# Two small bias arrays in front of x in place of in front of the slope: 64 bytes of shift for x, both weight halves, the stage and the identity

## What is computed

```python
Wc = conv_w[:, :, 0, 4]
def step(prev, x_i):
    y = jnp.einsum('oc,nch->noh', Wc, prev) + conv_b[None, :, None]
    y = jnp.where(y >= 0, y, prelu_a * y)
    cur = y + x_i
    return (cur, cur)
x = jnp.moveaxis(feature, 3, 0)
_, fwd_rest = jax.lax.scan(step, x[0], x[1:])
fl = jnp.concatenate([x[0:1], fwd_rest], axis=0)
_, bwd_rest = jax.lax.scan(step, fl[-1], fl[:-1], reverse=True)
```

## The kernel before

| tensor | remainder by 128 | remainder by 512 |
|---|---|---|
| `x_sb`, `w_hi` (and `pairs` in its place), `w_lo` (and `w_raw`), `stage`, `ident` | 0 | 128 |
| `a_scale`, `a_shift`, `g_scale`, `g_shift` | 0 | 128, 256, 384, 0 |
| `s_hi`, `s_lo`, `act_buf` | 64 | 320, 320, 320 |
| `unit`, `cent`, `gated_mean` (statistics) | 0 | 0, 256, 128 |
| `group_ones`, `ones_bf` | 96 | 96 |

## Time and profile before

### The profile page before, as it was taken

How to read it: one execution, slowest core, us unless ns; L and a number is a source line. 1 busy time by engine, 2 the same in 40 slices (tenths; PEclk the granted TensorE clock), 3 DMA queues, 4 the chain that set the end, 5 groups by cost and what they waited for, 6 DMA issues and landing times.

```text
span 852.3 us, 13842 instructions
## 1 busy us (share of the span) xinstructions
PE 828.0 (97%) x4060; PEld 661.3 (78%) x4060; DVE 660.5 (77%) x1461; ACT 421.1 (49%) x1401; POOL 66.7 (8%) x106
## 2 busy tenths in 40 slices
PE   7788899999999999999999999999999999999998
PEld 6743478888888888888888888888888888888887
DVE  6978877777767676676766788888888888888887
ACT  6874455444454445444454444544445444554445
POOL 8963300000000000000000000000000000000000
PEclk9999999999999999999999999999999999999999
DMA  9940200000000000000000023332333223332233
GB/s 381 417 193 0 100 26 0 1 0 0 0 0 0 0 0 0 0 0 0 0 0 0 15 84 98 98 91 62 94 98 98 82 65 98 98 98 73 75 98 99
DMA packets 70654, 56.34 MB, mean 66 GB/s; under 512 B 1904, under 2 KB 66416, under 8 KB 68720
## 3 DMA queue, kind: packets, MB, share of 16 engines
q1 hardware_dynamic: 70640, 56.17, 19.8%
HBM read 39.39 MB, written 16.78 MB: 66 GB/s over the span
## 4 chain that ended last, share of the span: by engine, by line
PE 87%; DVE 4%; DMA 3%; ACT 3%; SPq 1%; issue 1%; DVEq 0%; ACTq 0%
PE ps_prods L706 27%; PE ps_prods L700 26%; PE ps_prods L703 26%; PE ps_turns L722 6%; DMA x_sb<-x_cols 3%; SPq L306 1%; DVE below_flags L1061 1%; ACT stage L541 1%; ACT stage L517 1%; ACT ps_turns L481 1%; DVE cells L1078 0%; ACT w_hi L512 0%; PE ps_values L652 0%; ACT ps_prods L481 0%; PE ps_group L663 0%
## 5 line engine op out<-in xcount | busy, mean ns | idle before, releaser
L700 PE MATMUL ps_prods<-w_hi,s_hi 128*128 128x512 f32 x990 | 397.1, 401 | 0.0
L703 PE MATMUL ps_prods<-w_lo,s_hi 128*128 128x512 f32 x990 | 394.7, 399 | 0.0
L706 PE MATMUL ps_prods<-w_hi,s_lo 128*128 128x512 f32 x990 | 387.6, 392 | 0.0
L551 ACT ACTIVATE act_buf<-ps_prods 128x256 f32<-128x256 f32 x247 | 81.8, 383 | 338.1 <-PE ps_prods L706 333.0
L1167 DVE SCALAR_TENSOR_TENSOR x_sb<-act_buf,x_sb 128x256 f32 (+1 forms) x247 | 105.1, 426 | 143.7 <-ACT act_buf L558 133.7
L706 PEld LDWEIGHTS ps_prods<-w_hi,s_lo 128*128 128x128 f32 x990 | 186.4, 188 | 35.6
L700 PEld LDWEIGHTS ps_prods<-w_hi,s_hi 128*128 128x128 f32 x990 | 186.1, 188 | 33.5
L703 PEld LDWEIGHTS ps_prods<-w_lo,s_hi 128*128 128x128 f32 x990 | 186.5, 188 | 31.1
L558 ACT ACTIVATE act_buf<-ps_turns,bias 128x128 f32<-128x128 f32 x494 | 156.7, 376 | 49.5 <-PE ps_turns L722 49.5
L564 ACT ACTIVATE ps_below<-ps_turns,neg_bias 128x128 f32<-128x128 f32 x494 | 152.1, 361 | 0.0
L1174 DVE SCALAR_TENSOR_TENSOR x_sb<-ps_below,neg_slope,x_sb 128x256 f32 (+1 forms) x247 | 118.8, 481 | 5.4
(11 more groups left out here) (208 smaller groups left out, 369.2 us busy)
## 6 DMA issues: line engine op xcount, KB each, us to landing
stage<-x_cols SPq DMA_DIRECT2D x31, 512.0 KB, 3.9
out_cols<-x_sb SPq DMA_DIRECT2D x31, 512.0 KB, 4.6
x_sb<-x_cols SPq DMA_DIRECT2D x15, 1024.0 KB, 18.5
w_raw<-w_t SPq DMA_DIRECT2D x8, 512.0 KB, 19.1
x_sb<-x_cols SPq DMA_DIRECT2D x1, 2048.0 KB, 8.0
x_sb<-x_cols SPq DMA_DIRECT2D x2, 512.0 KB, 27.3
out_cols<-x_sb SPq DMA_DIRECT2D x4, 128.0 KB, 2.1
params<-gates SPq DMA_DIRECT2D x1, 60.0 KB, 14.2
```

The source lines that it names most:

```text
L551: act.activation(act_buf[:, half], ps_prod[c if bank is None else bank][:, half], ACT.Copy) .then_inc(raw_copied, 1)
L700: pe.matmul(out, s_hi[:, k, :], w_hi[:, k, w_cols], start=(k == 0), stop=False)
L703: pe.matmul(out, s_hi[:, k, :], w_lo[:, k, w_cols], start=False, stop=False)
L706: return pe.matmul(out, s_lo[:, k, :], w_hi[:, k, w_cols], start=False, stop=(k == CT - 1))
```

## The change

Two lines move: `bias` and `neg_bias`, 32 bytes per partition each, are allocated ahead of `x_sb` and no longer behind `g_shift`. Everything that lay between the two places starts 64 bytes higher: `x_sb`, `pairs`, `w_hi`, `w_raw`, `w_lo`, `stage`, `ident` and the four scale and shift arrays. What comes behind `neg_bias` (the slopes, all `tmp` tiles, `s_hi`, `s_lo`, `act_buf`) keeps its address. No instruction, wait, loop or transfer is added, removed or put elsewhere in its queue.

```diff
@@ -71,6 +71,8 @@
             return ctx.enter_context(nc.semaphore(name))
 
 
+        bias = sb("bias", [P, CT])
+        neg_bias = sb("neg_bias", [P, CT])
         x_sb = sb("x_sb", [P, CT, COLS, NH])
         pairing = ExitStack()
         pairs = pairing.enter_context(nc.sbuf_tensor("pairs", [P, 4 * C + P], fp32))
@@ -87,8 +89,6 @@
         a_shift = sb("a_shift", [P, N, CT])
         g_scale = sb("g_scale", [P, N, CT])
         g_shift = sb("g_shift", [P, N, CT])
-        bias = sb("bias", [P, CT])
-        neg_bias = sb("neg_bias", [P, CT])
         slope = sb("slope", [P, 1])
         neg_slope = sb("neg_slope", [P, 1])
         rest_slope = sb("rest_slope", [P, 1])
```

## The result

| | before | changed |
|---|---|---|
| median | 854.12 us (4 runs) | 863.46 us (862.14 to 863.55, 4 runs) |
| profiled execution | 854.0 us | 862.14 us |
| span | 852.3 us | 860.4 us |
| TensorE busy | 828.0 us | 835.8 us |

The change makes the kernel slower by 1.05% (ratio 1.0105, 95% interval 1.0092 to 1.0118). The forecast was 854.1, range 853.3 to 855.4. The profiled execution of the changed kernel is the shortest of its four: it is 8.1 us longer than the one before, where the medians are 9.3 apart. What follows accounts for the 8.1; the other 1.2 us no trace shows.

A forecast was written before the change was run, and what follows sets the result against it. The prediction took TensorE's count of scan matmuls by their distance as the bound. All four terms were zero (DMA -0.31 to +0.35, moving side -1.24 to +1.24), so it forecast the median, 854.1 us, range 853.3 to 855.4.

The forecast's parts named there:

- What bounds the kernel: In the 62 scan steps, some 738 us, time is the count of matmuls by their distance, 229 ns each.
- TensorE, stationary side: Weight loads and warm-up matmuls: remainders and a different distance between the operands cost zero; loads take 188 ns at each remainder.
- TensorE, moving side: Scan matmuls reading weights now at remainder 64: zero, bounded by a 0.42 ns clock pulse each, 1.24 us either way.
- The bf16 row: Nearest trace row: ones_bf at remainder 96, 216 ns between matmuls, so an off-line moving start costs at most 2 to 3 ns.
- the unexplained 13 ns: In each scan matmul, 229 ns is 13 ns more than bf16's 216; the trace doesn't say of what, taken as zero.
- Rival A: Slower: each of 2970 scan matmuls pays for a split line of the moving read; 856.6 from two pulses; chance 0.07.
- Rival C: Faster: the 192 over 512 start suits the scan's moving read better, 851.6 or less from two pulses; chance 0.07.
- Rival B: Slower: load pieces of x cut finer, deciding from 1.7 us or 19 ns a piece; 856 to 857; chance 0.04.
- VectorE, GpSimd, ScalarE: Their accesses to x, stage, state and w_lo cost zero at any remainder; L1142 stays at 426 ns.
- DMA: Load of x: zero, with -0.31 to +0.31 us for 64 bytes (2.4 ns) a piece; last store 0.04 us.
- The rule weighed in the prediction: Load of x: transactions start on multiples of 256 bytes, so the shift wastes two more beats, 0.31 us, giving 854.4.
- The cover of 0.34 us a step: In the scan, the path through ScalarE and VectorE may grow 0.34 us a step before TensorE waits.

The follow-up runs named there:

- e2_x_not_w: Kernel before with bias and neg_bias ahead of x_sb, slopes ahead of w_hi: x at remainder 64, weights at 0 by 128; 866.24 us, ratio 1.0139.
- e4_state_too: Changed kernel with a 64-byte gap ahead of s_hi, so weights and state keep the distance of the kernel before; 854.37 us, ratio 1.0.
- first probe: Kernel before plus 48 groups of 40 float32 matmuls of 512 columns behind the warm-ups, operand starts varied; 226.7 to 234.1 ns a matmul.
- second probe: Kernel before plus 25 groups of 40 matmuls with varied operand offsets, types and columns; bf16 216 ns, plain float32 112 ns a matmul.

## Why the prediction was wrong, point by point

*What bounds the kernel.* Right. The time is the number of matmuls by the time between their starts: 12.033 less 11.907 us a step explains 7.8 of the 8.1 us of the profiled executions.

*TensorE, stationary side.* Here is the step that failed: "The price of a different distance between the operands is zero by these rows." I named the very quantity and dismissed it by 188 against 188 ns and 394 against 395. Those are durations, and durations did not move in the slow kernel either. The fault is one that the front of this text warns of: the rate is in the starts. Nor was "the scan's stationary operand does not move anyway" a reason: its distance to the moving one did. Nor could the eight warm-ups have told. They lie at distance 0, the best one, but behind the first their starts are 225 to 236 ns apart, 231.5 in the mean, more than the scan's 229 at distance 64; a stream may need its first six matmuls to settle.

*TensorE, moving side.* This is the term of the sum that was mis-sized: I took zero with bounds of one clock pulse, 1.24 us, and it was 7.8 us. The 3.4 ns between 228.9 and 232.3, eight pulses, act on the 40 of a step's 48 matmuls that stand apart from the transposes: 0.136 us, against the 0.126 by which the step grew, so the rest of the step, around the transposes, gives a little back. The bf16 row was no neighbour: bf16 is indifferent to what costs float32 up to 7.4 ns. And the unexplained 13 ns over the bf16 distance were the hint: two of them go away at distance 0 in the probe.

*Rival A* had the place (each matmul of the scan), the sign of the result and its mark in the profile (steps of 11.92 us or more, all else in place), at a chance of 0.07. Its cause, a split line of the moving operand, is refuted by e2_x_not_w and e4_state_too. *Rival C* was right that the present layout is not the best, by 0.5%, but the moving operand's own start is not what counts, and the place that C named, 192 over 512 with the state where it is, is the slower one. *Rival B* has a slip in its price: the load is 128 pieces in a row, so 1.7 us would be 13 ns a piece and not 19.

*VectorE, GpSimd, ScalarE.* Right where seen: L1142 stays at 426 ns, and L439's median goes from 907 to 910, 0.07 us over its 24 instructions. The argument for VectorE was empty, though: a fixed part and a price per column, drawn from two instructions, fit any two durations. It is the 426 ns with x moved and the state not that show it.

*DMA.* Small, within the bounds. ScalarE's start after the load of x moved from 39.24 to 39.37 us:

```profile
11.27 27.94 DMA x_sb<-x_cols
...
39.37 1.24 ACT ps_turns L481 x2
```

The 8 KB pieces have a median of 309 ns in the trace's records in each of the seven scan layouts with x at remainder 0 by 128, and 312 in each of the four with x at 64. That is near the 2.4 ns of the prediction's 64 bytes. But the means (316.5 to 319.0 against 318.2 to 319.6) overlap, and over the eleven kernels the end of the load varies by more than 0.31 us from layout to layout (39.08 to 39.56), so its worth on the path is not resolved. The rule weighed in the prediction ("DMA: Bandwidth & Descriptors", "How a descriptor splits into AXI transactions", in the Trainium skill) would have given, by the estimate there, 0.31 us, and these runs speak neither against it nor surely for it.

The Trainium skill, "TensorE: Matmul & The Clock Gate", section "Step-by-step: what each phase is for", says that the weight load has an SBUF read port of its own and takes no bandwidth from the running matmul. The first probe doesn't fit that for one-pass float32: with the other engines still, the same matmuls stand 226.7 to 234.1 ns apart by nothing but the distance of their operands. Here the measurement decides: the two reads are not indifferent to each other. For bf16, at 216 ns throughout, the second probe shows nothing against the page.

*The cover of 0.34 us a step* for ScalarE and VectorE was not used: TensorE has no gap in the scan of the changed kernel, but for its ends.

## What to carry to other kernels

Where TensorE streams 512 float32 columns in the one-pass form with a new stationary operand for each matmul, place the two operands so that their starts are equal modulo 256 bytes, the stationary operands of transposes in between included; with another number of columns, measure first. An edit of allocation order alone moved this kernel by nearly 2% (849.9 to 866.2 us), so keep the remainders fixed when other changes are compared. And read a stream's price from the distance of its starts, over more matmuls than it needs to settle, never from durations.

## What the runs showed that I had not expected

- A stream of one-pass float32 matmuls of 512 columns takes 226.7 ns at distance 0 modulo 256, 228.9 at 64, 232.6 at 128, and 233.2 to 234.1 at the other multiples of 32; bf16 takes 216 at all.
- With 256 columns the order turns: 119.8 ns at distance 0, 117.8 at 192 and 64.
- Such a stream can take six matmuls of 229 to 236 ns to settle at distance 0; with both operands 64 bytes in, two groups of the first probe settled after the first. An alternating one can settle at 228.3 in one place and at 236.7 in another.
- The kernel before with an empty gap of 64 bytes ahead of the state takes 849.9 us, less than both kernels.
